# One product less per context piece: the last keys' tile stacked with its own low parts

## What is computed

```
query = hidden_states @ Wq
keyt  = enc @ Wk
valt  = enc @ Wv
hs    = mha(query, keyt, valt)          # 8 heads, softmax over 718 keys
ca_q2 = mha(ca_q1, residual, residual) @ Wq
ca_hs2 = mha(ca_q2, ca @ Wk_ca, ca @ Wv_ca)
out   = (hs + ca_hs2) @ Wout + b_out + residual
```

## Time and profile before

| | us |
|---|---|
| median of 3 runs | 1011.73 |
| lowest, highest | 1010.91, 1013.59 |
| the profiled execution | 1011.86 |
| its span, first to last instruction | 1010.1 |

### The profile page before, as it was taken

How to read it: one execution, slowest core, us unless ns; L and a number is a source line. 1 busy time by engine, 2 the same in 40 slices (tenths; PEclk the granted TensorE clock), 3 DMA queues, 4 the chain that set the end, 5 groups by cost and what they waited for, 6 DMA issues and landing times.

```text
span 1010.1 us, 20729 instructions
## 1 busy us (share of the span) xinstructions
PE 988.2 (98%) x6740; PEld 959.7 (95%) x6740; DVE 677.8 (67%) x1129; ACT 489.2 (48%) x895; POOL 343.7 (34%) x286
## 2 busy tenths in 40 slices
PE   9999899999999999999999999999999999999998
PEld 8998799999999999999999999999999999998997
DVE  6445586767776767676767776777767676766444
ACT  7434455454554545454636363645454545446110
POOL 5212253334242515161615243343333343406000
PEclk9999999999999999999999999999999999999999
DMA  7989967787879777879697878787787877795354
GB/s 264 255 298 272 250 154 198 157 201 168 189 167 195 169 191 171 183 176 186 169 186 184 187 176 190 178 184 187 166 201 162 199 169 190 156 219 160 98 177 148
DMA packets 154169, 190.12 MB, mean 188 GB/s; under 512 B 80928, under 2 KB 108192, under 8 KB 154144
## 3 DMA queue, kind: packets, MB, share of 16 engines
q1 hardware_dynamic: 147456, 177.44, 73.5%
q10 hardware_dynamic: 6688, 12.35, 3.7%
HBM read 81.56 MB, written 19.95 MB: 100 GB/s over the span
## 4 chain that ended last, share of the span: by engine, by line
PE 78%; DMA 7%; SPq 5%; DVE 4%; issue 2%; ACT 2%; POOL 1%; ACTq 0%; DVEq 0%; POOLq 0%
PE psS L750 20%; PE psB L785 19%; PE psB L790 9%; PE psS L725 7%; PE psT L766 6%; PE psS L894 6%; PE psT L812 4%; PE psT L818 2%; SPq L382 2%; DMA kstack<-kT 2%; DMA enc_raw<-in_encN_dram 1%; SPq L379 1%; PE psB L867 1%; PE psB L844 1%; PE psT L819 1%
## 5 line engine op out<-in xcount | busy, mean ns | idle before, releaser
L750 PE MATMUL psS<-encT_keep,Wk_keep 128*128 128x360 f32 x1440 | 253.8, 329 | 0.0
L750 PEld LDWEIGHTS psS<-encT_keep,Wk_keep 128*128 128x128 f32 x1440 | 237.4, 188 | 1.1 <-issue 0.4
L785 PE MATMUL psB<-PT_h,encN_h 120*128 120x400 f32 x576 | 202.3, 351 | 0.0
L785 PE MATMUL psB<-PT_l,encN_h 120*128 120x400 f32 x576 | 198.8, 345 | 0.0
L1133 ACT ACTIVATE probs<-psS,negmax 100x718 f32<-100x718 f32 x128 | 110.2, 861 | 133.5 <-DVE negmax L1524 133.4
L612 POOL TENSOR_TENSOR encT_keep<-encT_raw,encT_keep 128x718 fp32r<-128x718 f32 x45 | 79.7, 1772 | 199.6 <-ACT encT_keep L1162 197.3
L1548 DVE TENSOR_TENSOR kT<-psS,kT 128x718 fp32r<-128x718 f32 x80 | 72.4, 905 | 85.7 <-ACT kT L1157 85.6
L620 POOL TENSOR_TENSOR encN_l<-enc_raw,encN_h 120x768 fp32r<-120x768 f32 x48 | 93.1, 1940 | 90.9 <-ACT encN_h L1169 89.9
L790 PE MATMUL psB<-PT_h,encN_l 120*128 120x400 f32 x576 | 120.3, 344 | 0.8 <-POOL encN_l L620 0.8
L603 POOL TENSOR_TENSOR Mbd<-Mbd,fmask 128x320 fp32r<-128x320 f32 x48 | 46.7, 973 | 218.0 <-DMA Mbd<-m_split 215.4
L1157 ACT ACTIVATE kT<-psS 128x718 fp32r<-128x718 f32 x80 | 61.7, 771 | 115.7 <-PE psS L750 102.5
(11 more groups left out here) (245 smaller groups left out, 1642.2 us busy)
## 6 DMA issues: line engine op xcount, KB each, us to landing
kstack<-kT SPq DMA_DIRECT2D x64, 448.8 KB
kstack<-kT SPq DMA_DIRECT2D x192, 112.2 KB
enc_raw<-in_encN_dram SPq DMA_DIRECT2D x48, 360.0 KB, 5.5
encT_raw<-in_encT_dram SPq DMA_DIRECT2D x45, 359.0 KB, 4.4
kstack<-kT SPq DMA_DIRECT2D x32, 359.0 KB
kstack<-kT SPq DMA_DIRECT2D x32, 269.2 KB
kstack<-kT SPq DMA_DIRECT2D x32, 179.5 KB, 3.2
kstack<-kT SPq DMA_DIRECT2D x64, 89.8 KB, 3.5
```

Of the source, the lines that this page charges most:

```text
L750: mm = pe.matmul(keys_in(f, first)[:, half, 0:HALF], w[:, c, f * 128:(f + 1) * 128], e[:, c, k0:k0 + HALF], start=(j == 0), stop=(j == 3 * ...
L785: pe.matmul(psB[:, 1, 0:RH], eN[0][:, k, cc], PT[p][:, k, rows], start=(k == 0 and p == 0), stop=False)
```

## The change

Key rows are tiled as 5 full tiles of KP = 128 and a last tile of TAIL = 78 (718 = 5 x 128 + 78). The last tile's 50 free rows are used to stack: with TH = 39, rows 78 to 116 of the last tile hold a second factor pair, so that two products over 117 rows do what three over 78 rows would:

- product A: `eN[0]` (rows 0..77 context high, rows 78..116 context low of rows 0..38) with `PT[0]` (rows 0..77 probabilities high, rows 78..116 the high of rows 0..38 again).
- product B: `eN[1]` (rows 0..77 context high again, rows 78..116 context low of rows 39..77) with `PT[1]` (rows 0..77 probabilities low, rows 78..116 the high of rows 39..77).

A piece has 5 x 3 + 2 = 17 products. The doubled rows come about so:

- `norm` (DVE) has a third instruction: it multiplies columns 640..678 of the head's probabilities into columns 718..756, with a wait behind it, ahead of the multiply of all 718. The transposes then turn these columns along, so `PT[0]` has its doubled rows without a further step.
- `tail_pt(b, half)` (ACT queue, two DMAs a batch): `PT[0]` rows 39..77 to `PT[1]` rows 78..116, after `pt_low` of the half's last head.
- `enc_twice(b)` (ACT, after `enc_high(b, 0)`): the high part of the last tile again, into `eN[1]`.
- `enc_low` (POOL): 4 subtractions for 3. The first, of the last tile, writes over `enc_raw`; it waits for `enc_twice`. `load_enc(b, 0)` now brings the last two tiles.
- `tail_enc(b)` (SP queue, two DMAs a batch): context low rows out of `enc_raw` into `eN[0]` and `eN[1]`.

In a piece the low product of tile 4 now comes first among the low ones, and the two stacked products last. `wo_low(2)` of batch 15 moves behind `enc_low`. Waits that counted by 3 count by 4.

```diff
-KP = (KEYS + KT - 1) // KT
+KP = 128
 KPAD = KT * KP
-HALF = KPAD // 2
+HALF = 360
+FULLK = KEYS // KP
+TAIL = KEYS - FULLK * KP
+TH = TAIL // 2
+TSTK = TAIL + TH
...
+        tail_low = enc_raw[0:KP, FULLK * C:KT * C].bitcast(F32R)
...
+        def third(c):
+            return slice(4, 6) if c == 0 else slice(2 * (c - 1), 2 * c)
...
+                def tail_enc(b):
+                    wait_apart(sp, s["encN"], LOWS * b + 1, s["passed_sp"])
+                    for p in range(2):
+                        sp.dma_start(raw(eN[p][TAIL:TSTK, FULLK, :]), raw(tail_low[p * TH:(p + 1) * TH, :]))\
+                          .then_inc(s["entail"], 16)
...
                         load_q(i + 1)
-                    else:
+                    tail_enc(i)
+                    if not first:
                         wait_apart(sp, s["hsp"], 2 * i, s["passed_sp"])
                         load_v2(i)
...
                 def enc_low(b):
+                    pool.wait_ge(s["encNhi"], LOWS * b + 2)
+                    nc.gpsimd.tensor_tensor(tail_low, rawN[:, FULLK, :], eN[0][:, FULLK, :],
+                                            ALU.subtract).then_inc(s["encN"], 1)
...
-                for c in range(3):
+                for c in range(2):
                     wo_low(c)
                 enc_low(B - 1)
-                for c in range(3, FT):
+                for c in range(2, FT):
                     wo_low(c)
...
-                    for k in range(KT):
+                    for k in range(FULLK):
                         for p in range(2):
                             pe.matmul(psB[:, 1, 0:RH], eN[0][:, k, cc], PT[p][:, k, rows],
                                       start=(k == 0 and p == 0), stop=False)
-                    for k in range(KT):
-                        if u == 0 and k % KQ == 0:
-                            pe.wait_ge(s["encN"], PARTS * i + k // KQ + 1)
-                        mm = pe.matmul(psB[:, 1, 0:RH], eN[1][:, k, cc], PT[0][:, k, rows],
-                                       start=False, stop=(k == KT - 1))
-                    mm.then_inc(s["u"], 1)
+                    for n, k in enumerate((4, 0, 1, 2, 3)):
+                        if u == 0 and n in (0, 1, 3):
+                            pe.wait_ge(s["encN"], LOWS * i + (n + 1) // 2 + 2)
+                        pe.matmul(psB[:, 1, 0:RH], eN[1][:, k, cc], PT[0][:, k, rows], start=False, stop=False)
+                    if u == 0:
+                        pe.wait_ge(s["entail"], 32 * i + 32)
+                    if c == 0:
+                        pe.wait_ge(s["pttail"], 32 * i + 16 * half + 16)
+                    pe.matmul(psB[:, 1, 0:RH], eN[0][0:TSTK, FULLK, cc], PT[0][0:TSTK, FULLK, rows],
+                              start=False, stop=False)
+                    pe.matmul(psB[:, 1, 0:RH], eN[1][0:TSTK, FULLK, cc], PT[1][0:TSTK, FULLK, rows],
+                              start=False, stop=True).then_inc(s["u"], 1)
...
+                def enc_twice(b):
+                    nc.scalar.activation(eN[1][0:TAIL, FULLK, :], rawN[0:TAIL, FULLK, :], ACT.Copy)\
+                      .then_inc(s["encNhi"], 1)
+                def tail_pt(b, half):
+                    act.wait_ge(s["ptlo"], HEADS * b + 4 * half + 4)
+                    rows = slice(half * RH, (half + 1) * RH)
+                    act.dma_start(raw(PT[1][TAIL:TSTK, FULLK, rows]), raw(PT[0][TH:TAIL, FULLK, rows]))\
+                      .then_inc(s["pttail"], 16)
...
-                    dve.wait_ge(s["inv"], HEADS * i + h + 1)
+                    dve.wait_ge(s["inv"], 2 * (HEADS * i + h) + 1)
+                    nc.vector.tensor_scalar(P[h % PRING][0:S, KEYS:KEYS + TH],
+                                            P[h % PRING][0:S, FULLK * KP:FULLK * KP + TH], inv[:, h:h + 1],
+                                            None, ALU.mult).then_inc(s["inv"], 1)
+                    dve.wait_ge(s["inv"], 2 * (HEADS * i + h) + 2)
```

More of the change, by code:

```diff
@@ L109, in program @@
         NP = FT + 1
+        LOWS = PARTS + 1
         HALFCOLS = slice(GT, 2 * GT)
@@ L256, in program @@
         stage1_stores = "qst0 qst1 qst2 qst3a qst3b v2st mst0 mst1 mst2"
-        names = " ".join((loads, products_done, exps_and_highs, steps_and_lows, splits, stage1_loads, stage1,
+        names = " ".join((loads, products_done, exps_and_highs, steps_and_lows, splits, tails, stage1_loads, stage1,
                           stage1_stores)).split()
@@ L362, in load_enc @@
                 def load_enc(b, c, first=False):
-                    free("encN", PARTS * (b - 1) + c + 1, first)
-                    ks = slice(c * KQ, (c + 1) * KQ)
+                    free("encN", LOWS * (b - 1) + c + 2, first)
+                    if c == 0:
+                        free("entail", 32 * b, first)
+                    ks = third(c)
                     sp.dma_start(rawN[:, ks, :], encN[bass.ds(b, 1)].rearrange("o (k p) c -> p (o k) c", p=KP)[:, ks, :])\
@@ L547, in _ @@
                 batch(B - 1, last=True)
-                sp.wait_ge(s["encN"], PARTS * B)
+                sp.wait_ge(s["encN"], LOWS * B)
                 for t in range(2):
@@ L1349, in batch @@
                         enc_high(i, 0)
+                        enc_twice(i)
                     if last:
@@ L1356, in batch @@
                         enc_high(i, 0, first)
+                        enc_twice(i)
                         store_q3(5)
+                    tail_pt(i, 0)
                     if not last:
@@ L1394, in batch @@
                     pt_high(i, 7)
-                    if not last:
+                    if last:
+                        tail_pt(i, 1)
+                    else:
                         u_high(i, 1)
+                        tail_pt(i, 1)
                         expo(i + 1, 0)
```

18 lines of the change are left out of this document (12 added, 6 removed).

## The result

| | before | after |
|---|---|---|
| median, us (20 runs each, taken together) | 1014.71 | 1019.96 |
| ratio to before, 95% interval | | 1.0052 [1.0037, 1.0068] |
| profiled execution, us | 1011.86 | 1021.25 |
| its span, us; mean granted clock | 1010.1; 0.994 | 1019.5; 0.983 |

What follows compares the result with a forecast made beforehand. The prediction took the kernel as bound by TensorE (matmul engine busy 98%). Terms -17.6 + 6.0 - 0.5 + 4.0 + 1.0 = -7.1 us, from 1011.9 to 1004.8 us; range 996 to 1012, held at about 0.8.

Steps and rivals of the forecast that it cites:

- Matmuls removed: All context pieces: one product less in 6 pieces of 16 batches, 96 x 0.183 = -17.6 us; stacked products cost the same.
- Small multiply: VectorE, each norm: 128 extra 39-column multiplies, 0.22 to 0.28 us each, taken as 0.25; 32 us, mostly beside TensorE's work.
- (a): values(i, 0) waiting for u_low(i, 2) on VectorE: stalls about 0.40 us in each of 15 meetings, +6.0 us (3.5 to 7.5).
- Other norms have idle time on VectorE behind them: VectorE behind the other norms: idle time, as with 0.91 us before u_low at 516.04; no cost was added.
- The port: VectorE and GpSimd share it: the instruction that starts first goes first; norm(5) gets through or waits 1 us less.
- rival 2: At norm(3) the long multiply loses to GpSimd, 2 us late; 14 batches x 0.95 = +13.3, 1018 us. Chance 0.13.
- Loop transfers "hidden by 3 us": tail_enc on SP's queue lands at 552, stacked products come at 555.3; load_v2 and lift(i+1, 0) behind it not late.
- ScalarE at nothing: enc_twice (0.5 us a batch) and two DMA issues (0.3 to 0.5 each) on ScalarE, costed at nothing in the loop.
- (b): turn(i, 4) waiting for hs_add(i-1, 1): most of the 0.2 us lost per batch goes, late ones worsen; -0.5 us (-2.5 to +3).
- Batch 0, +4.0: Batch 0: tail_enc stands behind load_q(1), so u0 stalls before its stacked products; +4.0 us (2 to 6), once.
- Last batch, +1.0: Last batch: u0 waits for enc_low's four subtractions, +0.7, and +0.3 for norm(7) before tile(0, 0); +1.0 us (0 to 2.5).

Runs made afterwards that it cites:

- the mended kernels that keep the small multiply: Kernel after; fourth encN subtraction waits for norm(i, 6), tail_enc(0) before load_q(1), u_low(i-1, 2) before b2_norm(i): 1004.09 us; also first tail_pt behind expo(i, 6): 999.68 us.
- the wait on GpSimd alone: Kernel after with one wait added: in the loop GpSimd's fourth subtraction of encN waits for norm(i, 6). Measured 1018.71 us, 1.0048 of the kernel before.

## Why the prediction was wrong

**Matmuls removed: right.** 11 + 6 products at 0.183, stacked ones too; the weight loads of the loop fell by 15.7 us.

**Small multiply: its length right, its places wrong.** Free of GpSimd it takes 0.25, as taken. At (a) the forecast's +6.0 was 0.40 a batch. In the kernel after it does not show. With the other stall mended it came to 0.57 over before (0.87 against 0.30): the mechanism was right, the term was too small by 0.17 a batch. Where norm(0) was free of GpSimd it was the size that was forecast (0.67 against 0.30). The chain of the working, "without a gap" from 515.46 on, has 0.91 us of idle time before u_low at 516.04, as its own say; it is full from there on. The step that failed is the sentence "Other norms have idle time on VectorE behind them", by which 0.25 us costs nothing anywhere but at (a). It was argued from one norm. Behind norm(6) stands k_low(i+1, 0), and behind that SP's queue. The runs showed there, in place of nothing, a small multiply that took 1.45 us for 0.25 in 14 of 14 batches, q 1.4 us later, and 15.7 us of stalls at the two scores.

**The port: rule right, cases missed.** That order of starts decides is borne out: 0.16 us ahead was enough, 0.43 behind cost 1.2. At 0.01 apart the rows don't tell who was first. The rule was applied to norm(3), norm(5) and hs_add, and norm(3) came out as forecast (0.39 and 0.60, so rival 2 did not happen). The long multiply of norm(5) was forecast under 1.3 and took 1.41, that of norm(1), not gone through either, 0.99 in all 14 where it had been 0.60. norm(6) was not gone through, though it stood 0.16 us ahead of a subtraction and 0.25 was about to be put in front of it. The Trainium skill's rule that a length of 39 takes the two-port mode too (VectorE: DVE Perf Modes, "Mode 2×_2P — use both read ports for one tensor") agrees with the rows: 1.44 us beside GpSimd, 0.25 alone.

**Loop transfers "hidden by 3 us": right for what they carry, wrong for the queue.** No stacked product waits in the loop. But "what is queued behind is load_v2 and lift(i+1, 0), and neither is late" stopped one step short: load_q(i+1) and lift(i+1, 1) stand behind lift(i+1, 0), and q landed 1.4 us ahead of its use. k_low's 0.86 us of delay went with 1.4 at q, and the use comes 0.4 earlier. The added transfers are not it, since without them q lands as late (19.9); why the delay grows on the way stays open.

**ScalarE at nothing: wrong in batch 0.** Issues of 0.3 to 0.5 were taken from rows of other transfers; these take 0.77 to 0.81 on ScalarE (1.39 the first time) and 0.75 to 0.84 on SP. Moving the first one behind `expo(i, 6)` took 2.6 us off the halt at b2_scores2.

**(b), -0.5: right.** The distance at turn(i, 4) went from 0.54 to 0.50. The four turns behind keys together lost 0.32 us a batch before, 0.28 after; in the mended kernels that keep the small multiply they lose 0.44 to 0.50.

**Batch 0, +4.0: the halt right (3.7 us), the batch wrong (+6.3 where +2.9 was forecast).** Missing were the halt at b2_scores2 (3.1 for 1.7) and the granted clock, 0.90 over the batch where it was 0.97: a halt costs its own length and the loads behind it at the lower level. How much of the 3.4 us between the two is scatter is not known: with the wait on GpSimd alone, which leaves batch 0 as it is, it took 71.23 us for 68.48, and in the kernel before 60.25 for 62.21. **Last batch, +1.0:** less the products, -0.1 was forecast, and it came to +2.9. u0 did not halt before its last products, but the weight load of b2_xm came 3.3 us behind the last turn's and not 1.0. That distance is 0.9 to 5.4 us in all these kernels, with and without the change; its cause stays open.

**The sum of the loop.** Forecast -15.4 + 6.0 - 0.5 = -9.9 us; measured -3.1. The difference of 6.8 is 15.7 us at the two scores, less the 7.7 that (a) did not cost (6.0 forecast and 1.7 that before lost there), less 1.2 elsewhere. Rival 2 had the right kind, a race on the port lost through the small multiply, but the wrong norm; that its 1018 us is near the measured time is luck, since the multiply of norm(3) took 0.60 and the stall that it counted did not come.

## What to carry to other kernels

An instruction put into every turn of a helper has to be followed at every one of its places: for each, who is next on the engine, and what stands in the queues behind that. Where two engines share a port, list every pair of starts within the size of the edit; 0.25 us here moved one by 1.2 us, and in the kernel before, in all norms, the time by 32. And a stall that is found first hides the next one: after mending one, look for the other on the same batch before putting a price on the repair, and compare the mended new kernel with an equally mended old one.
